# Layers' attention in steps of all sixteen heads, on sixteen 32x32 tiles of the array

## The reference

```python
qkv = x @ Wqkv                      # x: 4 x 512 x 128, Wqkv: 128 x 3072
q, k, v = sixteen heads of 64, per head
q = l2norm(q) * qs; k = l2norm(k) * ksc   # then rotary tables on both
# windows of 32 tokens; a query window sees its own and the previous 32 keys
sim = einsum('bhwie,bhwje->bhwij', bq, bk2) * 8.0
sim = where((i < j) | (i > j + 32) | (j == -1), -max, sim)
out = einsum('bhwij,bhwje->bhwie', softmax(sim, -1), bv2)
return out.reshape(b, n, 1024) @ Wo
```

## Time and profile before

| What | us |
|---|---|
| median of 3 runs | 2531.78 (2521.78 to 2538.67) |
| span of the profiled execution | 2515.4 |
| PE, DVE, ACT, POOL busy in it | 2362.9, 1744.7, 1598.6, 1463.1 |

### The profile page before, as it was taken

How to read it: one execution, slowest core, us unless ns; L and a number is a source line. 1 busy time by engine, 2 the same in 40 slices (tenths; PEclk the granted TensorE clock), 3 DMA queues, 4 the chain that set the end, 5 groups by cost and what they waited for, 6 DMA issues and landing times.

```text
span 2515.4 us, 122084 instructions
## 1 busy us (share of the span) xinstructions
PE 2362.9 (94%) x53677; PEld 1738.9 (69%) x53677; DVE 1744.7 (69%) x3537; ACT 1598.6 (64%) x5036; POOL 1463.1 (58%) x1408
## 2 busy tenths in 40 slices
PE   9958999999999999999999999999878999999967
PEld 8836777777777777777777777777645666666657
DVE  4477888888878888878787888887335555555534
ACT  3226777777777787777777877777625444545422
POOL 1166667656666667666666677665117656566307
PEclk9979999999999999999999999999979999999978
DMA  4013333333333334333333343333216222222136
GB/s 91 15 33 86 85 78 96 95 80 85 93 88 94 81 83 103 92 83 81 88 95 85 79 97 82 84 92 84 57 22 185 48 48 48 48 48 48 30 95 250
DMA packets 230210, 204.62 MB, mean 81 GB/s; under 512 B 133687, under 2 KB 155464, under 8 KB 229552
## 3 DMA queue, kind: packets, MB, share of 16 engines
q1 hardware_dynamic: 225296, 190.91, 30.6%
q0 software_dynamic: 2208, 5.58, 0.6%
q10 hardware_dynamic: 2176, 0.33, 0.1%
HBM read 86.05 MB, written 15.70 MB: 40 GB/s over the span
## 4 chain that ended last, share of the span: by engine, by line
PE 72%; DVE 17%; issue 4%; SPq 2%; ACT 2%; DMA 1%; POOL 1%; POOLq 0%; ACTq 0%; DVEq 0%
PE psum L1208 8%; PE psum L1226 6%; PE psum L1955 5%; PE psum L1234 5%; PE psum L1109 5%; PE psum L1934 5%; PE psum L1940 4%; PE psum L1111 4%; PE psum L1110 3%; DVE kT L1443 3%; PE psum L1989 3%; PE psum L1979 3%; DVE rotated L1418 3%; PE psum L1185 2%; PE psum L1216 2%
## 5 line engine op out<-in xcount | busy, mean ns | idle before, releaser
L1354 ACT ACTIVATE p<-p,stat 128x64 f32<-128x64 f32 x1536 | 512.5, 336 | 40.1 <-DVE stat L1490 38.0
L1573 POOL TENSOR_TENSOR p<-p,inverse 128x512 f32<-128x512 f32 x192 | 200.2, 1043 | 465.9 <-DVE inverse L1493 464.9
L1208 PE MATMUL psum<-kT,qT 32*32 32x64 f32 x24576 | 306.7, 223 | 30.3 <-issue 29.1
L2088 DVE TENSOR_REDUCE largest<-psum 128x1 f32<-128x512 f32 x256 | 165.0, 686 | 228.0 <-PE psum L1940 228.0
L1208 PEld LDWEIGHTS psum<-kT,qT 32*32 32x32 f32 x24576 | 264.0, 103 | 82.2 <-issue 81.1
L1354 ACT ACTIVATION_READ_ACCUMULATOR p<-p,stat 128x1 f32 x1536 | 288.6, 188 | 0.0
L1418 DVE SCALAR_TENSOR_TENSOR rotated<-psum,scales,rotary 128x512 f32<-128x512 f32 x384 | 271.1, 742 | 24.3 <-ACT sq L1290 24.2
L1552 POOL TENSOR_TENSOR sq<-sq 128x512 f32<-128x512 f32 x192 | 245.1, 1276 | 42.4 <-ACT sq L1290 42.1
L1290 ACT ACTIVATE sq<-psum 128x512 f32<-128x512 f32 x384 | 212.8, 581 | 63.3 <-PE psum L1139 45.9
L1226 PEld LDWEIGHTS psum<-pT,v_win 64*64 64x64 f32 x12288 | 197.3, 135 | 47.6 <-issue 40.6
L1109 PE MATMUL psum<-xs,wqkv_high 128*128 128x512 f32 x384 | 204.9, 534 | 24.3 <-DVE rotated L1418 24.3
(11 more groups left out here) (352 smaller groups left out, 5448.6 us busy)
## 6 DMA issues: line engine op xcount, KB each, us to landing
v_win<-v_tok SPq DMA_DIRECT2D x576, 128.0 KB
rnorm_wide<-rnorms SPq DMA_DIRECT2D x384, 64.0 KB
v_win<-v_tok SPq DMA_DIRECT2D x336, 64.0 KB
q_rows<-q_rows_all SPq DMA_DIRECT2D x32, 512.0 KB, 4.6
tile_weights<-expert_table SPq DMA_DIRECT2D x23, 512.0 KB, 6.1
wqkv<-L_ffn_Wqkv SPq DMA_DIRECT2D x96, 64.0 KB, 2.4
rel_values<-sq SPq DMA_DIRECT2D x60, 64.0 KB, 2.2
wo<-L_ffn_Wo SPq DMA_DIRECT2D x48, 64.0 KB
```

Source lines behind the costliest of these rows:

```text
L1208: last = PE.e.matmul(psum[WIN * blk:WIN * (blk + 1), f, out], q[rows, g, half, tok:tok + WIN], k[rows, g, half, tok:tok + 2 * WIN], start= ...
L1354: last = A.e.activation(p, p, ACT.Exp, bias=t.stat[:, h, 2 * g + f:2 * g + f + 1], accum_out=t.sum[:, h, g, f:f + 1])
L1573: G.e.tensor_tensor(p, p, t.inv[:, h, :, :].unsqueeze(3).to_broadcast([P, GROUPS_TF, 2, 2 * WIN]), ALU.mult).then_inc(*t.p_scaled.by(m))
```

## The change

- A step of attention takes a whole tile with all 16 heads. `PARTS`, `part_*` become `TILES_TF`, `tile_*`, one step every eight rounds from round 39.
- Scores use all four row groups (one bank each, banks 0 to 3), 128 products (256 matmuls in the profile) in one step on sixteen array tiles. The masks are sixteen 32x32 products of 256 columns in the same array tiles, before the scores.
- Transposes go to banks 0 and 1, weighed values to banks 2 and 3, so that scores of tile n wait for the copies of n-2, and the transposes of n for `keep` of n+1.
- `keep`, the largest, the scaling and both copies work on 1024 columns at a time instead of 512, half as often. The 16 exponentials are spread over five rounds.
- Value steps are at rounds 30 and 34 (before 29 and 31), value windows from round 36 (before 31). Wo comes in four DMAs instead of eight. Two splits of weights are at other rounds.

```diff
-PART_FIRST = 39
-PART_AT = {"score": 0, "keep": 0, "largest": 1, "exp": 2, "inverse": 3, "scale": 3, "turn": 5, "turn_copy": 6, "weigh": 6, "o_copy": 8, "mix": 9, "add": 9}
-VALUE_FIRST, WINDOWS_AT = 29, 31
+TILE_FIRST = 39
+TILE_AT = {"score": 0, "keep": 0, "largest": 1, "inverse": 7, "scale": 7, "turn": 10, "turn_copy": 11, "weigh": 12, "o_copy": 13, "mix": 14, "add": 15}
+EXP_AT = {2: range(0, 3), 3: range(3, 6), 4: range(6, 9), 5: range(9, 12), 6: range(12, HEADS)}
+VALUE_FIRST, VALUE_STEPS_AT, WINDOWS_AT = 30, (0, 4), 36
-SPLIT_AT = {2: 13, 3: 31, 0: 39, 1: 40, 4: 56, 5: 59}
+SPLIT_AT = {2: 13, 3: 31, 0: 39, 1: 40, 4: 59, 5: 60}
...
+def tile_tensor(c, t, n, s):
...
+    if s == TILE_AT["score"]:
         PE.wait_ge(*t.k_scaled.on((u, GROUPS_TF - 1)))
         PE.wait_ge(*t.made.on((u, 2 * GROUPS_TF - 1)))
+        if n:
+            PE.wait_ge(*t.scores_kept.on(n - 1))
+        if n >= 2:
+            PE.wait_ge(*t.pt_kept.on(n - 2))
+            PE.wait_ge(*t.o_kept.on(n - 2))
+        for blk in range(TPB):
+            for j in range(4):
+                rows, to = slice(HALF_D * j, HALF_D * (j + 1)), slice(WIN * blk, WIN * (blk + 1))
+                mask = t.maskb[rows, 0 if i == 0 and blk == 0 else 1, :].unsqueeze(1).to_broadcast([WIN, GROUPS_TF, COLS])
+                PE.e.matmul(psum[to, j, 0:GROUPS_TF * COLS].rearrange("p (g k) -> p g k", g=GROUPS_TF), c.identb[rows, rows], mask, start=True, stop=False)
         for g in range(GROUPS_TF):
             for half in range(2):
                 for blk in range(TPB):
...
+                    for j in range(4):
                         rows = slice(HALF_D * j, HALF_D * (j + 1))
+                        last = PE.e.matmul(psum[WIN * blk:WIN * (blk + 1), j, out], q[rows, g, half, tok:tok + WIN], k[rows, g, half, tok:tok + COLS],
                                            start=False, stop=(half == 1 and g == GROUPS_TF - 1))
+    if s == TILE_AT["turn"]:
+        PE.wait_ge(*t.p_scaled.on(n))
+        if n + 1 < TILES_TF:
+            PE.wait_ge(*t.scores_kept.on(n + 1))
...
+def tile_scalar(c, t, n, s):
+    if s in EXP_AT:
+        A.wait_ge(*t.biased.on(n))
+        for h in EXP_AT[s]:
...
+    if s == TILE_AT["turn_copy"]:
+        A.wait_ge(*t.turned.on(n))
```

More of the change, by code:

```diff
@@ L735, in rounds @@
         now = [("spread", b, 0) for b in NORM_SCALE if r == NORM_SPREAD] + [("scale", b, 0) for b, at in NORM_SCALE.items() if r == at]
[L736 to L739, removed]
+        for n in range(TILES_TF):
+            s = r - UNIT * (n // TPB) - TILE_FIRST - TILE * (n % TPB)
+            if 0 <= s < TILE_STEPS:
+                now.append(("tile", n, s))
         for u in range(UNITS_TF):
@@ L801, in transformer_setup @@
     t.v = [sb(f"v_win{i}", [P, TPB, PAIRS, DH]) for i in range(2)]
-    t.stat, t.sum, t.inv = sb("stat", [P, 2, 2 * GROUPS_TF]), sb("sum", [P, 2, GROUPS_TF, 2]), sb("inverse", [P, 2, GROUPS_TF, 2])
-    t.p, t.pt = [sb(f"p{i}", [P, GROUPS_TF, 2, 2 * WIN]) for i in range(2)], [sb(f"pT{i}", [P, GROUPS_TF, P]) for i in range(2)]
-    t.ot = [sb(f"oT{i}", [P, GROUPS_TF, P]) for i in range(2)]
+    t.stat, t.sum, t.inv = (sb(n, [P, 2, HEADS]) for n in ("stat", "sum", "inverse"))
+    t.p, t.pt, t.ot = [sb(f"p{i}", [P, GROUPS_TF, 4, COLS]) for i in range(2)], sb("pT", [P, PAIRS, P]), sb("oT", [P, PAIRS, P])
     t.sq, t.sqf, t.xc = c.sq4[0:2], c.sq4[2], c.sq4[3]
-    tiles, parts, units, layers = range(UNITS_TF * TPB), range(UNITS_TF * PARTS), range(UNITS_TF), range(DEPTH)
+    tiles, units, layers = range(TILES_TF), range(UNITS_TF), range(DEPTH)
     per = lambda name, over, many: Signal(nc, "tf_" + name, [(n, k) for n in over for k in many])
@@ L841, in ring_takes @@
 def ring_takes(kind, n, s):
-    if kind == "part":
-        return ["mix"] * (s == PART_AT["mix"] and n % 2)
+    if kind == "tile":
+        return ["mix"] * (s == TILE_AT["mix"])
     users = []
@@ L859, in ring_freed @@
 def ring_freed(t, kind, n, user):
-    if kind == "part":
-        return t.z_mixed.on(n // 2)
+    if kind == "tile":
+        return t.z_mixed.on(n)
     if user == "rn":
@@ L893, in early_sync @@
     for blk in range(4):
-        rows, first = slice(blk * WIN, (blk + 1) * WIN), blk % 2 * WIN
-        SP.e.dma_start(t.mask[rows, :, :], io["c_mask"][rows, :, first:first + 2 * WIN]).then_inc(*t.once.by(1 + blk))
+        rows = slice(blk * WIN, (blk + 1) * WIN)
+        SP.e.dma_start(t.mask[rows, :, :], io["c_mask"][0:WIN, :, 0:COLS]).then_inc(*t.once.by(1 + blk))
     for j, n in enumerate(("k_scale", "q_scale")):
@@ L964, in value_windows @@
     if n >= 2:
[L965 removed]
+        SP.wait_ge(*t.weighted.on(n - 2))
     k = 0
@@ L1186, in feed_tensor @@
         last.then_inc(*t.f_down.by(u))
-def part_tensor(c, t, m, s):
-    PE, psum, (n, h) = c.PE, c.psum, divmod(m, 2)
+def tile_tensor(c, t, n, s):
+    PE, psum = c.PE, c.psum
     u, i = divmod(n, TPB)
     q, k, v = t.q[u % 2], t.k[u % 2], t.v[n % 2]
-    if s == PART_AT["score"]:
+    if s == TILE_AT["score"]:
         PE.wait_ge(*t.k_scaled.on((u, GROUPS_TF - 1)))
         PE.wait_ge(*t.made.on((u, 2 * GROUPS_TF - 1)))
[L1196 to L1200, removed]
+        if n:
[8 more added lines that the diff above has]
+                PE.e.matmul(psum[to, j, 0:GROUPS_TF * COLS].rearrange("p (g k) -> p g k", g=GROUPS_TF), c.identb[rows, rows], mask, start=True, stop=False)
         for g in range(GROUPS_TF):
@@ L1375, in early_vector @@
     V.e.tensor_reduce(t.by_half[:, :], c.ident[:, :].rearrange("p (j f) -> p j f", j=4), AX, ALU.add).then_inc(*own.up())
-    V.e.tensor_copy(t.maskb[:, :, :], t.mask[:, 0:1, :].to_broadcast([P, 2, 2 * WIN])).then_inc(*own.up())
+    for first in range(2):
+        V.e.tensor_copy(t.maskb[:, 1 - first, :], t.mask[:, first, :])
     V.wait_ge(*own.now())
-    V.e.tensor_copy(t.maskb[0:WIN, 0, :], t.mask[0:WIN, 1, :])
     for kind in range(2):
@@ L1528, in transformer_pool @@
         for kind, n, s in now:
-            if kind == "part":
-                part_gpsimd(c, t, n, s)
+            if kind == "tile":
+                tile_gpsimd(c, t, n, s)
             elif kind == "unit":
```

178 lines of the change are left out of this document (81 added, 97 removed).

## The result

| | before | after |
|---|---|---|
| median, us | 2531.40 (2521.78 to 2538.67) | 3318.26 (3306.07 to 3322.14) |
| span of the profiled execution | 2515.4 | 3318.9 |

The ratio is 1.311, with a 95% interval of 1.306 to 1.315: 31% slower, 787 us, against 3145 forecast and a range up to 3330. In the new kernel masks are L1204, scores L1211, transposes L1220, weighing L1230, mixing L1238, sums L1138, one projection half L1108 to L1110, `keep` L1486, the largest L1491, the key scaling L1445, the value copy L1307, the exponentials L1356.

A forecast was written before the change was run, and what follows sets the result against it. The prediction took TensorE, the fullest engine in the layers, as the bound. Its terms, -72 + 144 + 182 + 361 = +615 us, on the profiled 2515.4 plus 16, gave 3145 us, range 2780 to 3330.

The forecast's parts named there:

- (d): Rival: every tile's value windows come late, not one in four; 3 us more on each tile, 3435 us; chance 0.10.
- scores, masks, weighing: TensorE's attention matmuls: sixteen array tiles keep the old matmul pace; gain 0.75 us a tile, 72 us.
- stops of the stream: Score steps: TensorE stops for its next block of 256 instructions; 2.0 us a tile against 0.51, +144 us.
- order and shared banks: Weighing, mixing, transposes: TensorE waits on ACT's step order and shared banks; +1.9 us a tile, 182 us.
- value windows: SP's DMA queue: tile 2's window loads wait behind the norms' third spread; 15.7 us a unit, 361 us.
- lower clock: TensorE after the window wait: idling drops it to 1.2 GHz; 3 us so lose 1.5, within the windows' 15.7.
- (c): Rival: the array sets the scores' pace and instructions keep up; 195 us gained, ending at 2337 us; chance 0.08.
- (a): Rival: value windows come in time, through unseen SP slack or a harmless blocked copy; 2785 us; chance 0.13.

The follow-up runs named there:

- e3: The changed kernel without the score products of the first half of each head's features, 128 score matmuls a step instead of 256: 3042.8 us.
- e9: e1 with each tile's scores in two bursts two rounds apart, no product left out: 2907.9 us.
- e4: The changed kernel with a tile's exponentials in steps 3 to 6, four each, so ACT's turn copy comes first: 3338.8 us.
- e5: The changed kernel with the edits of both e1 and e4: 3077.4 us.
- e1: The changed kernel with the norms' third and fourth spreads at unit rounds 25 and 26 instead of 19 and 24: 3036.4 us.
- e2: The kernel before with only the new rounds for value steps, value windows and two weight splits; old attention steps: 3098.5 us.
- e7: e6 without the score products of the first half of each head's features: 2764.8 us.
- e6: e5 with the value steps at rounds 32 and 34 instead of 30 and 34: 3063.9 us.
- e12: e9 with the value steps at rounds 32 and 34 instead of 30 and 34: 2986.8 us.
- e10: e9 with bursts by banks, and `keep` and the largest in halves of 512 columns: 2948.0 us.
- e8: The kernel before without the score products of the first half of each head's features: 2491.6 us.
- e11: The kernel before with only its masks changed, to eight 32x32 products a part in the scores' array tiles: 2540.8 us against 2532.4.

## Why the prediction was right, and where it was off

The measured 3318 lies in the range, 173 us above the forecast; the case was the forecast's own, not (d). That it lies in the range is in part luck: the clock and the stops, as they came out, would alone have made 3145 + 23 x (8.9 + 2.3) = 3403, over the top of 3330, and the order term, taken too large, made up for it. Term by term, in us a unit:

| term | forecast | measured |
|---|---|---|
| scores, masks, weighing | -3.0 | about -3 |
| stops of the stream | +6.0 | about +8 |
| order and shared banks | +7.6 | about +4 |
| value windows | +14.2 | +13.5 |
| lower clock | +1.5 | about +10 |

- **Pace of the scores, weighing.** Right: 10 to 11 ns a matmul on sixteen tiles, as on eight (e3); masks 0.12 us (0.15), weighing 2.00 us from start to next start (2.0). Rival (c) falls. The factor of 10.6 of the Trainium skill ("TensorE: Matmul & The Clock Gate", Part 3) is not reached by products of 64 columns with a load each; the runs show no 512-column case.
- **Stops.** Right in kind, somewhat low in size. Idle on "issue" before scores is 8.3 us a unit against 1.1, and a step's busy time, 181.9/57 = 3.2 us a tile, hides up to another 0.5 a tile of stops, 2.0 a unit, where before it hid 0.9 (269.7/169 - 1.48 in each of eight parts): 7.2 + 1.1 = 8.3. The step was taken at 2.0 us a tile and is about 2.5. e3, e9 and the counts in multiples of 256 show the cause. "Mostly hidden" (the Trainium skill, "Runtime: NRT & Kernel Launch", Instruction fetch mechanics) is contradicted by 166.6 us of them in 2100.
- **Order and shared banks.** The term of 1.9 us a tile failed in its largest part: the wait for the turn copy was 0.1 instead of 1.1, mixing 0.3 instead of 0.5, transposes 0.02 instead of 0.3; e4 and e5 show that nothing is won there. What PE waits besides is feed-forward: 2.7 us a unit for ACT's square (L1163). The idle that is neither stop nor value copy is 27.2 - 8.3 - 12.7 - 0.8 (L1179 for the value copy) = 5.4, less the old 0.8 that was not "issue" before scores: 4 to 5.
- **Value windows.** Right, chain and price: 12.7 + 0.8 = 13.5 us a unit. e1 and e2 show the cause from both sides. Rival (a) falls. So does (d): ACT's copy waits in three of four tiles (61 times in 20.4 units), but of PE's 41 waits behind it 21 are 10.6 to 12.3 us long, one a unit as forecast, and the other 20 are 0.3 to 1.9 us.
- **Clock.** This is the mis-sized term. I let each long wait cost 1.5 us of slow clock. The mean of 0.84 in 250 to 1700 us means 0.32 of the stretch at 1.2 GHz; with PE busy 0.74 of the time and half of that lost, that is 0.12 of 102.8, 12 us a unit by a rough reading. PE's busy time gives the same: 75.7 where 67.2 - 3.0 = 64.2 are due, 11.5 more, of which 1.1 are short stops; 10.4 stay. I had read one long gap and priced it once a unit, where gaps now come in every tile. The trace tells the two apart: from 500 to 1700 us, 11.7 units, 382 us stand at 1.2 GHz and PE is busy in 277 of them, but only 59 of the 277 lie in slow stretches that touch a gap of over 8 us. If half the clock doubles the time of the work, half of the 59 is lost: 2.5 us a unit, near the 1.5 that I gave the long gap. The other 218, by the same reckoning 9.3 us a unit, lie elsewhere, among stops and waits of 1 to 3 us, whose clock the prediction put at nothing. With the measured sizes the forecast becomes 3145 + 23 x (8.9 clock + 2.3 stops - 3.6 order - 0.7 windows) = 3304, against 3318. As the clock's size is what the others leave over, this checks the account and not each size.

What is **left open**: e9 is still 376 us over before; by the spans, (2906.0 - 2515.4)/23 = 17.0 a unit of 86.0. From the table, PE idles 14.1 us a unit in it (before 1.8) and is busy 71.9 (before 67.2): 12.3 + 4.7. Of the 197 us idle in the table's stretch 39.5 are stops; the rest is in many waits of up to 3.5 us for ACT and DVE steps of other parts of the unit, as in e7. Moving value steps (e6, e12), exponentials (e4, e5) or halving DVE steps (e10) moved these waits and did not remove them. I think that rounds written for small steps hand over badly when steps are twice as long, with the second bound of e8 so near; no run shows that by itself. Nor does any show what decides the clock: e10 idles no more than e9 (186 against 197 us of 1200) and has 0.90 against 0.95, though more of its idle is in gaps of over 2 us (62 against 48 us).

## What to carry to other kernels

When a step moves by a few rounds, follow each in-order queue that it passes, SP's DMA issues first: one spread that waits for DVE, standing ahead of ten window loads, cost more than all that was done to the matmuls. Merging steps into longer bursts of tiny matmuls saved no TensorE time here, where they are paced by instructions, and a burst of two instruction blocks stops nearly every time, one of half the length in half of the cases (e9) or seldom (e3). And before forecasting from an engine that is 97% busy, price what a gap costs at the lower clock, in every place where the change makes one.

## What the runs showed of the hardware that was not expected

- A 10.66 us gap leaves PE at 1.2 GHz with work queued, and about a third of the new layers runs so although PE is busy three quarters of the time. In e8 PE idles 86 of 1200 us in short waits at a mean clock of 1.00.
- TensorE's stops come at whole multiples of 256 of its instructions, and they come back for very little: 12 instructions more in a burst of 260 turned 16 us of saved busy time into 15 us of stops (e11), while 2 x 128 products two rounds apart lost a third of what 256 in a row did (e9).
- Two 128x128 masks and the step to the first 32x32 product take 0.32 us from start to start, eight 32x32 masks 0.12 (e11). Of the 0.32, 0.12 is from the first mask to the second and 0.20 from the second to the first score; in e11 0.10 lie between the last mask and the first score. So about 0.1 us (estimate) is left for the change of shape.
- Ten window issues on SP took 6.3 us in the place shown, and 9.0 in the earlier trace rows, with nothing else issued between them in either.
